# Four transformer layers on one core: the set-up as 18 steps inside the stream order instead of a block with a barrier ahead of it

## What is computed

```python
# layer 0 (layer 2 has the same form, with _ln(context) in its cross attention)
mod = silu(cond) @ adaln_w + adaln_b          # six parts: shift, scale, gate, twice
x = x + g_sa * (attend(_ln(x) * (1 + sc_sa) + sh_sa) @ sa_proj_w + sa_proj_b)
x = x + attend(_ln(x), context) @ ca_proj_w + ca_proj_b
x = x + g_ff * (gelu(xm @ fc1_w + fc1_b) @ fc2_w + fc2_b)
# layer 1: cross attention to the context, both sides modulated by silu(cond) @ Wss
# layer 3: one-head attention to the context gives `evidence`, then
combined = concatenate([nx, evidence, anchor], axis=-1)       # anchor = cond
probs = softmax(combined @ router_W + router_b)
h = silu(combined @ e_w1 + e_b1)                              # three experts
routed = sum((h @ e_w2 + e_b2) * probs)
g = sigmoid(silu(combined @ gate_w1 + gate_b1) @ gate_w2 + gate_b2)
x = x + g * (routed @ out_w + out_b)
```

## Time and profile before

| | |
|---|---|
| median of three runs | 1866.98 us (1864.02 to 1872.07) |
| the profiled execution | 1866.06 us |
| its span | 1864.3 us |
| TensorE busy | 1756.0 us, 94% |
| VectorE busy | 1639.4 us, 88% |
| ScalarE busy | 1383.1 us, 74% |
| GpSimd busy | 643.9 us, 35% |
| transfers | 42.6 MB, 23 GB/s on average |

### The profile page before, as it was taken

How to read it: one execution, slowest core, us unless ns; L and a number is a source line. 1 busy time by engine, 2 the same in 40 slices (tenths; PEclk the granted TensorE clock), 3 DMA queues, 4 the chain that set the end, 5 groups by cost and what they waited for, 6 DMA issues and landing times.

```text
span 1864.3 us, 88096 instructions
## 1 busy us (share of the span) xinstructions
PE 1756.0 (94%) x38181; PEld 1502.5 (81%) x38181; DVE 1639.4 (88%) x4236; ACT 1383.1 (74%) x3340; POOL 643.9 (35%) x1145
## 2 busy tenths in 40 slices
PE   3788999999999999999999999999999999999898
PEld 3577788888788888888888888888888888877788
DVE  2898889899899999999999999989999989998874
ACT  1465678787778778777877787878777777777697
POOL 1432323333423333333333333333333333432341
PEclk9899999999999999999999999999999999999999
DMA  4200000000000000000000000000000000000000
GB/s 162 71 14 9 17 23 9 17 23 23 23 23 14 16 19 23 23 23 23 9 17 23 23 23 23 23 3 23 23 23 23 23 13 18 20 11 9 8 5 15
DMA packets 57165, 42.62 MB, mean 23 GB/s; under 512 B 13520, under 2 KB 55632, under 8 KB 56528
## 3 DMA queue, kind: packets, MB, share of 16 engines
q1 hardware_dynamic: 56784, 36.99, 6.8%
HBM read 32.51 MB, written 4.46 MB: 20 GB/s over the span
## 4 chain that ended last, share of the span: by engine, by line
PE 74%; DVE 14%; ACT 6%; issue 3%; DMA 0%; POOL 0%; SPq 0%; DVEq 0%; POOLq 0%
PE half L981 9%; PE half L881 8%; PE half L861 7%; PE half L900 7%; PE half L885 7%; PE half L928 5%; PE half L918 5%; DVE top L1070 4%; PE half L802 4%; PE half L990 4%; PE half L848 4%; PE half L911 3%; PE half L833 3%; PE half L837 3%; ACT pT L1246 2%
## 5 line engine op out<-in xcount | busy, mean ns | idle before, releaser
L761 POOL TENSOR_TENSOR shifted<-moments,eps 128x2 f32<-128x2 f32 x256 | 50.6, 198 | 1027.1 <-DVE moments L1037 1027.0
L1211 ACT ACTIVATE pT<-half 128x512 f32<-128x512 f32 x640 | 328.0, 610 | 102.3 <-PE half L885 101.2
L1070 DVE TENSOR_REDUCE top<-half 128x32 f32<-128x2048 f32 x160 | 365.1, 2282 | 29.4 <-PE half L861 27.8
L881 PE MATMUL half<-o_rows,of_keys 32*128 32x128 f32 x5120 | 273.8, 281 | 5.1 <-ACT o_rows L1163 3.0
L885 PE MATMUL half<-q_heads,k_heads 32*128 32x128 f32 x5120 | 261.4, 271 | 3.0 <-issue 2.9
L1246 ACT ACTIVATE pT<-half,mod 128x64 f32<-128x64 f32 x896 | 196.1, 332 | 50.6 <-PE half L981 49.5
L881 PEld LDWEIGHTS half<-o_rows,of_keys 32*128 32x128 f32 x5120 | 205.9, 186 | 26.3 <-issue 11.5
L885 PEld LDWEIGHTS half<-q_heads,k_heads 32*128 32x128 f32 x5120 | 207.8, 187 | 5.4 <-issue 5.4
L1191 ACT ACTIVATE k_heads<-half,key_bias,own_head_sb 128x256 f32<-128x256 f32 x320 | 163.4, 571 | 47.8 <-PE half L837 46.2
L861 PE MATMUL half<-k_heads,q_heads 32*128 32x128 f32 x5120 | 187.9, 281 | 9.5 <-issue 5.0
L1043 DVE TENSOR_SCALAR n_rows<-x_rows,moments,rstd 128x128 f32<-128x128 f32 x512 | 189.0, 416 | 3.9 <-POOL rstd L763 3.0
(11 more groups left out here) (151 smaller groups left out, 3745.0 us busy)
## 6 DMA issues: line engine op xcount, KB each, us to landing
gates<-gate_store SPq DMA_DIRECT2D x128, 128.0 KB, 3.1
x_rows<-x SPq DMA_DIRECT2D x32, 128.0 KB, 2.2
c_rows<-context SPq DMA_DIRECT2D x32, 128.0 KB, 2.5
out<-x_rows SPq DMA_DIRECT2D x32, 128.0 KB, 1.8
w_sb<-weights SPq DMA_DIRECT2D x1, 2368.0 KB, 12.7
pT<-weights SPq DMA_DIRECT2D x1, 1024.0 KB, 4.7
logit_bias<-logit_store SPq DMA_DIRECT2D x64, 1.5 KB, 3.4
row_sb<-rows SPq DMA_DIRECT2D x1, 769.5 KB, 6.4
```

The source lines that it names most:

```text
L881: nc.tensor.matmul(halves[HALF_OF[n]][:, g, tb * D:(tb + 1) * D], of_keys[part, 2 * tb:2 * tb + 2, :], low[s][part, :], start=True, stop=F ...
L1070: nc.vector.tensor_reduce(top[s][:, :].rearrange("p (g c) -> p g c", c=32)[:, :, 0:2 * GROUP], halves[HALF_OF[n]][:, :, :].rearrange("p g ...
L1211: nc.scalar.activation(turn_cols[s][:, g, :], halves[HALF_OF[n]][:, g, :], ACT.Exp, scale=ATT_SCALE).then_inc(scores_read, 1)
```

## The change

The set-up has no block of its own any more, and the barrier behind it is gone. Its work becomes 18 steps, `FOLDS`, which stand in `SEQUENCE` as the letter f between the digits; the digits themselves and `HALVES` are unchanged. The first two folds stand ahead of every stream's step, the last one after 90 stream steps. Each fold takes banks by the common plan and is counted with the steps around it. The products are the same; the mods are made four to a bank, the sum for cond is copied by ScalarE, and the key biases are made ahead of the loop. TensorE takes its first-layer weights under a wait of their own, `l0_weights_in`, and turn 0 waits for all weights. The first `load` steps copy only the first layer's mods; the rest is copied ahead of layer 1's norm.

```diff
+FOLDS = ([("cond", None), ("mods", 0), ("gates", None), ("bias_p", 0), ("mods", 1), ("mods", 2)] + [("turn", n) for n in range(3)]
+         + [("product", n) for n in range(4)] + [("e_b2", None), ("bias_p", 1), ("mods", 3), ("mods", 4), ("logits", None)])
+MODS_OF = [range(n, min(n + 4, M_COND)) for n in range(0, M_COND, 4)]
+BIAS_P_OF = [range(0, 2), range(2, len(ATTENTIONS))]
 SEQUENCE = (
-    "0241021000230020202221103203132032010100301132010410310242032021113100231014204130010200113000330240"
+    "ff02410210002300f202f0222f110f320313f203201f0100f301132f010410f31024203f202111f310023f1014f2041f3001"
...
+        "cond": (0, 1), "mods": (1, 0), "gates": (1, 0), "bias_p": (1, 0), "turn": (0, 1), "product": (0, 1), "e_b2": (1, 0),
+        "logits": (1, 0),
...
-                for tile, at, column, width in W_LOADS[1:]:
-                    sp.dma_start(tile_of(tile)[:, at:at + width], weights[:, column:column + width]).then_inc(weights_in, 16)
-                sp.wait_ge(weights_in, ALL_WEIGHTS)
...
-        nc.multi_engine_barrier(ENGINES, sems_to_clear=range(first_sem.num, last_sem.num + 1))
...
+                sp.dma_start(own_head[:, :], own_head_in).then_inc(small_in, 16)
+                load_weights(W_LOADS[0], 0, W_LOADS[0][3], mod_weights_in)
+                load_rows(0)
+                load_weights(W_LOADS[1], 0, L0_COLS, l0_weights_in)
+                load_rows(2)
+                sp.dma_start(gate_bias, rows[:, R_KEPT:R_COLS].rearrange("p (n k c) -> p n k c", k=3, c=D)[:, :, 2, :]).then_inc(gate_bias_in, 16)
+                sp.dma_start(row_sb[:, :], rows[:, 0:R_KEPT]).then_inc(rows_in, 16)
+                load_rows(1)
+                load_weights(W_LOADS[1], L0_COLS, W_LOADS[1][3] - L0_COLS, weights_in)
+
+                sp.wait_ge(v_emptied, used_by(FOLD_AT["gates", None], FOR_VECTOR))
+                sp.dma_start(gate_store, gate_rows[0:B, :]).then_inc(gates_stored, 16)
+                load_rows(3)
+                sp.wait_ge(gates_stored, 16)
+                for s in (0, 2, 1, 3):
+                    load_gates(s, 0, 0)
+                for load in W_LOADS[2:]:
+                    load_weights(load, 0, load[3], weights_in)
+                for s in (4, 5):
+                    load_rows(s)
+                    load_gates(s, 0, 0)
+
+                sp.wait_ge(v_emptied, used_by(FOLD_AT["logits", None], FOR_VECTOR))
+                sp.dma_start(logit_store, logit_rows[0:B, :]).then_inc(logits_stored, 16)
+                sp.wait_ge(logits_stored, 16)
                 for s in range(STREAMS):
-                    load_gates(s, 0, 0)
                     load_logits(s, 0)
...
+                    if kind == "turn":
+                        if arg == 0:
+                            pe.wait_ge(rows_in, 16)
+                            pe.wait_ge(weights_in, 16 * len(W_LOADS[1:]))
+                        dst = to_a.slot()
+                        for at in range(4):
+                            mm = nc.tensor.transpose(dst[:, at * D:(at + 1) * D], to_turn[4 * arg + at], ident[:, :])
+                        mm.then_inc(a_filled, 1)
+                        ready["turned", s] = to_a.moved_out()
...
+                            dve.wait_ge(v_emptied, used_by(FOLD_AT["mods", 0], FOR_VECTOR))
+                            copy_mods(n, 0, M_L1Q)
...
+                        if n == first_scores(3):
+                            act.wait_ge(gates_stored, 16)
+                        if n == first_scores(4):
+                            act.wait_ge(logits_stored, 16)
```

More of the change, by code:

```diff
@@ L215, in interleave @@
 def interleave():
-    done, order = [0] * STREAMS, []
-    for s in map(int, SEQUENCE):
-        order.append((*STEPS[done[s]], s))
-        done[s] += 1
+    done, folds, order = [0] * STREAMS, iter(FOLDS), []
+    for c in SEQUENCE:
+        if c == "f":
+            order.append((*next(folds), None))
+        else:
+            s = int(c)
+            order.append((*STEPS[done[s]], s))
+            done[s] += 1
+    assert next(folds, None) is None
     assert done == [len(GROUP_STEPS) * rounds for rounds in ROUNDS]
@@ L252, with first, first_scores, next_step @@
 CONTEXT_NORMS = context_norms()
+FOLD_AT = {(kind, arg): n for n, (kind, arg, s) in enumerate(ORDER) if s is None}
+def first(*kinds):
+    return min(n for n, (kind, _, s) in enumerate(ORDER) if kind in kinds and s is not None)
+def first_scores(s):
+    return min(n for n, (kind, _, t) in enumerate(ORDER) if kind == "scores" and t == s)
+def next_step(n):
+    return next(m for m in range(n + 1, len(ORDER)) if ORDER[m][2] == ORDER[n][2])
 CONTEXT_NORMS_EACH = len(CONTEXT_NORMS) // GROUPS
@@ new lines, in _ @@
+                    if kind == "product":
+                        after("turned", s)
+                        dst, at = to_a.slot(), 0
+                        for lhsT, rhs in product_banks[arg][0]:
+                            mm = nc.tensor.matmul(dst[:, at:at + rhs.shape[1]], lhsT, rhs, start=True, stop=True)
+                            at += rhs.shape[1]
+                        mm.then_inc(a_filled, 1)
+                        ready["folded", s] = to_a.moved_out()
+                    if kind == "e_b2":
+                        after("turned", s)
+                        dst = to_v.slot()
+                        for e in range(EXPERTS):
+                            mm = nc.tensor.matmul(dst[:, e * D:(e + 1) * D], turned[:, T_B2 + e, :], w("L3_out_w"), start=True, stop=True)
+                        mm.then_inc(v_filled, 1)
@@ L806, in _ @@
+                    if kind == "logits":
+                        nc.tensor.matmul(to_v.slot()[0:B, 0:EXPERTS], mods[:, M_COND, :], router(2), start=True, stop=True).then_inc(v_filled, 1)
                     if kind == "context":
@@ L932, in _ @@
                     if kind == "l3_query":
+                        if n == first("l3_query"):
+                            after("folded", None)
                         after("n", s)
```

341 lines of the change are left out of this document (169 added, 172 removed).

## The result

| | us (range, executions) | ratio to before, 95% interval |
|---|---|---|
| before | 1866.98 (1864.02 to 1872.07, 5) | |
| changed | 1855.80 (1851.83 to 1857.61, 5) | 0.9929 (0.9909 to 0.9950) |
| forecast | 1841.5 (1832 to 1849) | |

A forecast was written before the change was run, and what follows sets the result against it. TensorE was taken as the bound from 120 to 1600 us, with all gain in the set-up before: 37.3 - 2.2 - 2.1 - 1.3 - 1.3 - 1.3 - 3.6 = 25.5 us, giving 1841.5 us (range 1832 to 1849).

The forecast's parts named there:

- start: Set-up: without its waits and barrier, TensorE turns stream 0's first rows at 15.5 us instead of 52.80; lead +37.3 us.
- gates, first bias_p: Ahead of the first tops on TensorE: added records, mostly at half clock, cost 2.2 us; bounds 1.7 and 2.4.
- mods 1 and 2: Between top0 and top2: VectorE empties both mods' banks, eight instructions without a gap to hide them, costing 2.1 us.
- all products: Around TensorE's five gaps from 80.65 to 92.26 us: products of 3.4 us, of which 1.3 are paid; bounds 0 and 3.4.
- e_b2 to logits: Ramp folds: TensorE gets 3.6 us more, VectorE about 3.5, paid in full at 3.6 us; bounds 1 and 5.
- the extreme of rival 2: Set-up: a queue without landing order, third x near 19 us, gain 20.6 us, time 1846.4; chance 0.04 within rival 2.
- rival 2: Ramp: gates and last weights 3 to 7 us later, or third x at 16 to 19; 1845 to 1852 us; chance 0.23.
- Turn 0 and the late weights: At turn 0, near 35.1 us: wait for late weights costs 1.3 us, twelve turns another 1.3.
- gates 2 us later would not be covered: GpSimd before stream 3's rstd at 35.0 us: the weights wait covers half a microsecond, but not gates 2 us later.
- From there to the end: 0: After the logits folds: no lead lost, steps unchanged; some 12 us cover SyncE's held queue.
- Rival 1: Ramp: TensorE's 9.8 idle us hide the folds, returning up to 8 us; 1832 to 1836 us; chance 0.20.
- rival 4: Ramp: clock stays at 1.2 GHz, costing some 50 us; 1890 us, slower than before; chance 0.03.

The follow-up runs named there:

- e5: Changed kernel with late weight loads in the first burst, logits loads spread over streams, GpSimd's two lifts behind the fourth rstd; 1844.61 us, ratio 0.987.
- e2: Changed kernel with its eleven late weight loads issued in the first burst, ahead of the wait for gate rows; 1851.21 us, ratio 0.9898.
- e8: Changed kernel with logits reordered in DRAM, one 24-byte row per partition instead of two of 12, half the packets; 1849.05 us, ratio 0.9899.
- e3: Changed kernel with the twelve logits loads issued two at a time behind each stream's second gates' loads; 1848.06 us, ratio 0.9887.
- e6: Changed kernel with weights first and logits loads spread, plus four bursts of twelve unneeded 12-byte-row loads in the body; 1871.23 us, ratio 1.0021.
- e9: Changed kernel with all edits: weights first, logits loads spread, GpSimd's two products behind the fourth rstd, 24-byte logit rows; 1840.87 us, ratio 0.9860.
- e11: e5 again, unaltered, measured beside the kernel without the GpSimd edit; 1841.51 us, ratio 0.9865.
- c1: The kernel before, unchanged, for a second profile of it; 1866.79 us.

## Why the prediction missed

| step | forecast | measured, changed kernel |
|---|---|---|
| start | +37.3 | +37.7 |
| gates, first bias_p | -2.2 | -1.3 |
| mods 1 and 2 | -2.1 | -1.6 |
| late weights at turn 0, turns | -2.6 | -9.1 |
| products 0 and 1 | -1.3 (all products) | -1.0 |
| later products, e_b2 to logits | -3.6 | -5.1 |
| from there to the ninth reduction | 0 | -4.7 |
| from there to the end | 0 | -5.8 in one profile, -1.1 in its repetition |

**The start, gates and mods were right**, 1.8 us too cautious in sum. The start's bounds for the third x (13 to 19 us) held 13.8, so the extreme of rival 2, in which the transfers land together, did not occur. The start of 37.3 was forecast from the measured rate of 512-byte rows. The Trainium skill's page "DMA: Bandwidth & Descriptors", section "Specifications", puts line rate at 512 bytes and above. Worked out from that, as an estimate, the third x would have landed 1.3 us before the forecast 14.1, at 12.8; it landed at 13.8, so this trace does not bear it out. The 1.8 us were worth nothing in the changed kernel: the gate store was issued at 21.30 us, as forecast (21.2), and turn 0 waited for what is queued behind it.

**The step that failed first is "Turn 0 and the late weights".** The mechanism was named and the size was wrong: 6.91 us of wait instead of 1.3, beyond even its bound of 6, as its own line "I am wrong if turn 0 waits over 4 us" says. Three of its inputs were off. The weights' issues began at 29.41 and not 28.7 us. The 5.7 us for the eleven loads came from a place where they ran alone and had all been queued before; from 16 to 22 us the DMA engines moved 339 GB/s there. Here they were issued one by one, beside the gates' last rows, and from 30 to 40 us the engines moved 280 GB/s in all. And their last 384 rows of 512 bytes moved among the rows of x and context of stream 4, which came next in the queue. From the first issue to the last landing it was 10.9 us (29.41 to 40.35) and not 7.7 (28.7 to 36.4). TensorE came 1.6 us earlier than forecast as well (33.53 instead of 35.1), which makes the wait longer and costs nothing.

**The same step did not charge the clock.** The forecast had full clock from about 22 us on. The wait of 6.9 us took it to 0.50. From the second to the third reduction the changed kernel loses 9.1 us of lead and e5 1.4. Of the 7.7 between them 6.0 are idle time (6.91 against 0.96 that TensorE waits there in e5), so some 1.7 are the clock and smaller waits. A stop is dearer than its length; at 108 us it is 4.7 for 3.59.

**GpSimd was placed rightly and priced as covered.** Its rstd was forecast for 35.0 us and started at 35.19. The text let the wait for weights cover 0.5 us of it; it covered 3.2. Of the difference 1.8 us are VectorE, free at 32.75 and not at 34.5, and 0.7 the duration of rstd itself, which the text did not add to its start. The sentence "gates 2 us later would not be covered" priced the wrong change: the gates were not late, the better start lengthened VectorE's wait. With the weights on time this wait is the next, as e2 shows.

**"From there to the end: 0" failed at its first point.** The text looked at SyncE's held queue and found 12 us of cover for the next gates. The queue came free at 104.9 us and not at 97, and still GpSimd waited for no gates from 60 to 200 us, so that part was right. It did not ask what else the DMA engines carry. Before, the twelve loads had been issued in pairs between those of the gates, and TensorE had no such stop there. Moved behind the logits fold they run in one piece while TensorE starts 42 matmuls and weight loads per us, from 99.4 to 109.6 us; before, it was 22 from 53 to 60 us and 38 from 60 to 67. The price is 3.59 us of stop, 4.7 with the clock, shown by e8, e3 and e6. The rest of this term, the body, was right within what profiles can tell: -0.9 us on average over the ten of the table.

**The folds were slightly under-sized**: 6.1 us for products, e_b2, mods, bias_p and logits instead of 4.9, within the bounds of the two terms together (1 to 8.4).

**The rivals.** Rival 2 (loads late) had the right mechanism with 3 to 7 us (the last weights landed 4.0 us later than forecast), and alone would have given 1845 to 1852; it had 0.23. The stop at 108 us was none of the rivals, and with both the sum comes near the measured time: 1841.5 + 6.5 (turn 0) + 4.7 + 1.2 (folds) - 1.8 (start) = 1852.1, against medians of 1855.8 and 1853.3. Rival 1 (the ramp hides the folds) and rival 4 (half clock through the ramp) did not come. With both places mended, e9 and e11 take 1840.9 and 1841.5. That this meets the forecast of 1841.5 is in part luck: they have edits that the forecast did not know, e11 leads by 33.1 us at the third reduction instead of the forecast 30.4, and pays 6.4 instead of 4.9 from there to the ninth.

## What to carry to other kernels

When a load is moved, ask two things of it besides who waits for it: who shares the DMA engines at its new place, and how long its packets run by their number, not by their bytes. A cover ("this wait hides that one") is only as good as the two times it is made of, and a better start can lift it; list the second wait at the same point with its own size. A short stop of TensorE that the view calls "issue" in the midst of equal products is worth a look at the instruction packets of the same moment.

## What the runs showed of the hardware

- Rows of 12 bytes from DRAM to SBUF ran at about 106 per us over the 16 engines where they ran alone: 1,536 in 13.3 us in the changed kernel, for 18 KB. Rows of 256 bytes kept pace with their issue (1,536 in 7.9 us, 194 per us, issued in 8.1), rows of 24 bytes as well (768 in 8.6 us, issued in 8.4).
- While such a run lasted, TensorE's instruction packets were 10.2 to 12.7 us apart instead of the usual 3.8 to 8.8, and TensorE stopped for 3.59, 3.92, 2.15 and 0.29 us in four such places (108 us in the changed kernel, the first three bursts of e6). The Trainium skill's page "DMA: Bandwidth & Descriptors", section "Queues, rings and completion order", says that a DMA engine serves its queues in turn and switches only at the end of a packet of several descriptors. The traces agree in that the instruction queue is neither shut out for the whole run nor served at once: in the changed kernel its packet came at 109.6 us, 1.1 us before the last tiny row, and in e8 the packet of the same number came at 104.2. How many rows go by before it gets its turn no run here shows.
- Stops with no releaser, of 1.1 to 2.4 us and ended 2.2 to 2.8 us behind the start of an instruction packet (the stop of 3.59 us: 2.3), occur in the body of every profile here, in before too, in part at the same steps and in part at others. They are a part of what makes single profiles of one program differ by 2 to 4 us (c1).
